# Self-attention of a fused transformer block: the sum of the rotary embedding on GpSimd, V projected behind the cosines, and new orders for the stage

## What is computed

```python
def _rope(x, sin, cos):
    xe = x[..., ::2]; xo = x[..., 1::2]
    return jnp.stack((xe*cos - xo*sin, xe*sin + xo*cos), axis=-1).reshape(x.shape)

attn_in = _adaln(x, cond, ...)
q = _heads(attn_in @ wq); k, v = jnp.split(attn_in @ wkv, 2, axis=-1)
q = _rope(q, ...); k = _rope(_heads(k), ...)
a = softmax(einsum('bhnd,bhmd->bhnm', q, k) * DH**-0.5)
x = (heads_joined(a @ v)) @ wo + bo + x
```

## Time and profile before

| what | value |
|---|---|
| median of the runs | 2123.01 us |
| the profiled execution: its own time, its span | 2127.94 us, 2126.2 us |
| TensorE, VectorE, ScalarE, GpSimd busy over the span | 94%, 76%, 47%, 55% |
| the self-attention stage | from 34.03 us (first projection) to 438.86 us (last add) |
| granted TensorE clock over the program | 0.97 of full speed |

### The profile page before, as it was taken

The page is one execution under the profiler, slowest core; times in us unless marked ns, Lnnn a source line. Parts: engine busy times, 40 slices in busy tenths (PEclk is TensorE's granted clock), DMA queues, the critical chain, the costliest instruction groups (busy, mean ns, idle before and its releaser), DMA issues.

```text
span 2126.2 us, 53808 instructions
## 1 busy us (share of the span) xinstructions
PE 2008.8 (94%) x20816; PEld 1346.6 (63%) x20816; DVE 1622.6 (76%) x2362; ACT 990.0 (47%) x1606; POOL 1174.4 (55%) x721
## 2 busy tenths in 40 slices
PE   5899999879699999999999999999999999999987
PEld 2666667622166666666666766767666776776653
DVE  3788888836578888888887888888788887888832
ACT  2344444424244445445445545444554544554533
POOL 1344444400056667677677667667666766766760
PEclk8999999979799999999999999999999999999999
DMA  3522222100011111111111111111111111111100
GB/s 112 165 80 75 81 79 82 54 0 1 32 55 54 47 54 60 47 54 57 50 52 55 54 49 54 58 47 54 60 47 54 59 48 53 55 53 52 48 22 20
DMA packets 109750, 118.69 MB, mean 56 GB/s; under 512 B 26432, under 2 KB 74688, under 8 KB 109248
## 3 DMA queue, kind: packets, MB, share of 16 engines
q1 hardware_dynamic: 109504, 115.27, 16.4%
HBM read 36.52 MB, written 1.05 MB: 18 GB/s over the span
## 4 chain that ended last, share of the span: by engine, by line
PE 68%; POOL 13%; issue 11%; DMA 3%; DVE 3%; ACT 2%; SPq 0%; POOLq 0%; ACTq 0%; DVEq 0%
PE S L1089 18%; PE OB L1101 16%; PE PB L1036 8%; PE PB L1047 8%; PE S L1062 6%; POOL psum_acc L503 4%; POOL psum_acc L470 4%; POOL KL L463 4%; PE S L885 2%; PE PB L1110 2%; DMA qswapped<-qturned 2%; PE PB L1026 1%; PE PB L872 1%; PE PB L1120 1%; PE PB L1071 1%
## 5 line engine op out<-in xcount | busy, mean ns | idle before, releaser
L503 POOL TENSOR_TENSOR psum_acc<-psum_acc,P 124x1024 f32<-124x1024 f32 (+1 forms) x320 | 689.4, 2154 | 92.9 <-ACT P L628 75.1
L628 ACT ACTIVATE P<-S 124x1024 f32<-124x1024 f32 (+1 forms) x448 | 431.3, 963 | 465.9 <-PE S L1089 465.1
L817 DVE TENSOR_REDUCE mxc<-S 128x2 f32<-128x1024 f32 x384 | 469.1, 1222 | 89.4 <-PE S L1062 88.6
L1101 PE MATMUL OB<-P,V 124*64 124x256 f32 (+1 forms) x3328 | 429.4, 382 | 0.0
L496 POOL TENSOR_TENSOR psum_acc<-P 124x1024 f32<-124x1024 f32 x64 | 152.3, 2379 | 331.4 <-ACT P L628 331.4
L1101 PEld LDWEIGHTS OB<-P,V 124*64 124x64 f32 (+1 forms) x3328 | 224.5, 137 | 131.0 <-issue 40.8
L1089 PE MATMUL S<-QH,KH 64*124 64x256 f32 (+1 forms) x1664 | 254.2, 301 | 3.0 <-ACT P L628 3.0
L783 DVE TENSOR_TENSOR turned<-PB,rope 128x512 f32<-128x512 f32 (+1 forms) x256 | 146.0, 570 | 120.6 <-PE PB L1036 120.2
L1089 PE MATMUL S<-QL,KH 64*124 64x256 f32 (+1 forms) x1664 | 234.8, 277 | 0.0
L1089 PE MATMUL S<-MX,share 64*124 64x256 f32 (+1 forms) x1664 | 234.7, 277 | 0.0
L1089 PE MATMUL S<-QH,KL 64*124 64x256 f32 (+1 forms) x1664 | 234.5, 277 | 0.0
(11 more groups left out here) (118 smaller groups left out, 3241.2 us busy)
## 6 DMA issues: line engine op xcount, KB each, us to landing
swapped<-turned SPq DMA_DIRECT2D x512, 128.0 KB, 2.1
kv_w<-sa_kv_dram SPq DMA_DIRECT2D x64, 128.0 KB, 2.3
qswapped<-qturned SPq DMA_DIRECT2D x128, 64.0 KB, 1.9
kv_w<-ca_kv_dram SPq DMA_DIRECT2D x64, 96.0 KB, 2.2
ctxT_all<-ctxT_dram SPq DMA_DIRECT2D x8, 600.4 KB, 5.3
q_w<-sa_wq_dram SPq DMA_DIRECT2D x64, 64.0 KB, 2.0
q_w<-ca_wq_dram SPq DMA_DIRECT2D x64, 64.0 KB, 2.0
o_w<-ca_wo_dram SPq DMA_DIRECT2D x64, 64.0 KB, 2.1
```

The costliest lines, as they stand in the source:

```text
L503: pool.tensor_tensor(acc, acc, P_of(J, c)[0:rows, :, 0:w], ALU.add).then_inc(x.acc, 1)
L628: act.activation(P_of(J, c)[0:rows, :, 0:w], SP[0:rows, :, 0:w], ACT.Exp, scale=SCALE).then_inc(x.e, 1)
L817: dve.tensor_reduce(mxc[:, t, :, c:c + 1], MP[:, :, 0:w], AX.X, ALU.max).then_inc(x.am, 1)
L1101: ins = pe.matmul(OB[half(h), 0:N], Vb[J % 2][0:w, t, half(h)], P_of(J, c)[0:w, h, k * N:(k + 1) * N], start=(t == 0), stop=(t == len(a_.t ...
```

## The change

Three edits, all in self-attention:
1. The rotation's sum `r` leaves VectorE's list and becomes an instruction of GpSimd. `c` no longer works in place in PSUM: it writes its product from the bank into `QK[J % 2]` in SBUF, and takes over the wait for `l` of the step before the last, which frees that buffer. `r` then adds `swapped` to `QK` in place.
2. `v` waits for `c` of its step instead of `r`.
3. All tables but SyncE's are new. The projection leads by two iterations instead of three, `v` by one instead of two, `a` by one instead of two and `m` by none instead of one; the output product and its add lag by two instead of one.

```diff
     SELF = Stage("sa",
-                 "qk+3 sum+-1 p+-1 s v+2 a+2 m+1 o+-1",
-                 "r+2 am+1 t+3 rc+-1 dv+-1 c+3 ad+-1",
-                 "ve+1 mr h+2 oe+-1 e",
-                 "l+2 f",
+                 "qk+2 v+1 o+-2 m a+1 p+-1 sum+-1 s",
+                 "ad+-2 t+2 c+2 am+1 rc+-1 dv+-1",
+                 "ve+1 mr oe+-1 e h+2",
+                 "l+1 r+2 f",
                  "w+3 x+2")
...
+                def rotate(J, _):
+                    i = J % SLOTS
+                    wait(pool, z.c, J + 1)
+                    wait(pool, z.swap[i], J // SLOTS * 32 + 32)
+                    pool.tensor_tensor(QK[J % 2][:, :], QK[J % 2][:, :], swapped[i][:, :], ALU.add).then_inc(z.r, 1)
...
                 def cosines(J, _):
-                    wait(dve, z.t, J + 1)
-                    bank = halves(KB[J % 2][:, :])
-                    dve.tensor_tensor(bank, bank, both(ropeq[:, 0:N]), ALU.mult).then_inc(z.c, 1)
-
-                def rotate(J, _):
-                    i = J % SLOTS
-                    wait(dve, z.c, J + 1)
-                    wait(dve, z.swap[i], J // SLOTS * 32 + 32)
                     wait(dve, z.l, J - 1)
-                    dve.tensor_tensor(QK[J % 2][:, :], KB[J % 2][:, :], swapped[i][:, :], ALU.add).then_inc(z.r, 1)
+                    dve.tensor_tensor(halves(QK[J % 2][:, :]), halves(KB[J % 2][:, :]), both(ropeq[:, 0:N]), ALU.mult
+                                      ).then_inc(z.c, 1)
...
                 def project_v(J, _):
                     loaded(J)
-                    wait(pe, z.r, J + 1)
+                    wait(pe, z.c, J + 1)
```

More of the change, by code:

```diff
@@ L470, in fold @@
                     pool.tensor_tensor(added_up(J), P[:, :, 0:N], P[:, :, N:2 * N], ALU.add).then_inc(z.f, 1)
-                run_steps(SELF, in_order(SELF.pool, {"l": low_parts, "f": fold}))
+                run_steps(SELF, in_order(SELF.pool, {"r": rotate, "l": low_parts, "f": fold}))
             def cross():
@@ L757, in add @@
                         dve.tensor_tensor(x_b, x_b, XB[:, 0:N], ALU.add).then_inc(z.added, 1)
-                run_steps(SELF, in_order(SELF.dve, {"t": turn, "c": cosines, "r": rotate, "am": maximum,
+                run_steps(SELF, in_order(SELF.dve, {"t": turn, "c": cosines, "am": maximum,
                                                     "rc": invert, "dv": divide, "ad": add}))
```

## The result

The changed kernel takes 2111.76 us, the median of five runs (2104.18 to 2112.91), against 2122.61 for the kernel before (2121.08 to 2126.22): a ratio of 0.9941, with a 95% interval of 0.9921 to 0.9961. That is 10.9 us or 0.5% faster. The forecast was 2100.5 us, 22.5 us faster. The result lies outside the forecast's own range of 2095 to 2106 us and 0.24 us inside the end of the wide one, 2090 to 2112. Measured again on another occasion the kernel took 2113.56 us, ratio 0.9936 (0.9912 to 0.9960).

What follows compares the result with a forecast made beforehand. VectorE bounds the kernel at 5.19 us a step, TensorE 4% behind. Gains: 52 x 0.24 = 12.5, 7 x 0.72 = 5.0, fill 3, late copies 2, together 22.5 us: 2100.5 us against 2123.0; 8-in-10 range 2090 to 2112.

Steps and rivals of the forecast that it cites:

- TensorE's floor: Sum of TensorE's group distances in one self-attention step, start to start, kept for the new order: 4.91 us.
- The bank's loop: Shared bank's loop in a step, from maxima's rows through scores, products, sums, inverse and division to TensorE: 4.92 us.
- the exponential's: Loop in a step from scores through exponential, high parts behind it on ScalarE, and back to TensorE: 4.94 us.
- The signs that I had named: In the new profile: maxima 4.95 us apart, 9.2 at outputs, GpSimd's pass 1.28, TensorE above 97% of a 44 us batch.
- the signs of being wrong: Scores for the maximum regularly waiting for high parts, GpSimd's passes above 1.3 us, or a first batch not shorter.
- Late copies: Exchanged-row copies in self-attention: 0.28 us late at no cost, fifteen late ones give 2 us; bounds -3 and +4.
- The fill: Start of self-attention: the second step's turn no longer stands behind the first rotation; gain 3 us, between 1 and 5.
- The end: End of self-attention, where nothing overlaps: no change expected.
- Rival 1: Handovers between engines eat the gain: with 0.15 us more the step is 5.10 us, time 2109 us; chance 0.2.
- Rival 2: TensorE is no floor: the copy's loop decides the step at 4.81 us, 7 us more gain, 2093 us; chance 0.1.
- Rival 3: One bound exchanged for another: the step stays at 5.19 us, only the start of the stage gains, 2120 us; chance 0.07.
- Rival 4: VectorE and GpSimd's added pass take turns at SBUF: step 5.75 us, slower at 2159 us; chance 0.05.

Runs made afterwards that it cites:

- e_noinv: On `e_lead`, VectorE's inverse of the sums replaced by a multiplication with a column: 2088.78 us, ratio 0.9856 to the kernel before.
- e_nocopy: Changed kernel, but the rotation adds the turned tile and doesn't wait for the copy with exchanged rows, which still runs: 2093.97 us, ratio 0.9850.
- e_lead: Changed kernel with projection, turn, cosines and copy one iteration further ahead and a third QK buffer: 2097.13 us, ratio 0.9857 to the kernel before.
- after_again: The changed kernel, unchanged, measured once more on another occasion: 2113.56 us, ratio 0.9936 to the kernel before.
- e_dverot: Changed kernel with the rotation's sum back on VectorE, the new orders kept: 2133.66 us, ratio 1.0034 to the kernel before.
- e_oldorder: Changed kernel's edits 1 and 2 with the leads and order of the kernel before, only GpSimd's table changed: 2101.48 us, ratio 0.9901.
- e_fewer: On `e_lead`, one of the three products of the scores left out, 4 of a step's 16 matmuls: 2098.55 us, ratio 0.9902.

## Why the prediction was right, and where it was not

**Right.** VectorE set the step before, and the move freed it. TensorE's floor: forecast 4.91, measured 4.90 to 4.92 in `e_noinv`. The step: forecast 4.95, measured 4.95. The output step: 9.24, measured 9.23. GpSimd's pass: 1.28, measured 1.277 in the median; its handover to ScalarE: 0.05, measured 0.03. The bank's loop, forecast at 4.92, was mis-sized by 0.03 and sits on top instead of the exponential's: from the products to the sums it is 0.91 us and not 0.86, and the sums' matmuls take 0.60 and not 0.63. The forecast of 4.95 stood on the exponential's 4.94, so that it is exact to the hundredth is luck.

The signs that I had named came in part. One of the signs of being wrong came: the scores for the maximum waited for the high parts, 17 times and 14.4 us from 100 to 400 us. TensorE was not above 97% of a batch of 44 us; the best batch of the changed kernel is this one, 96.7%:

```profile
148.50:193.40 44.90, 43.41 (x480) 30.78 (x480) 37.54 (x42) 20.83 (x40) 30.23 (x24) 1.00 0.26 84
```

**Wrong, and the cause of the missing half: "Late copies".** I took +2 us, with -3 as the lower bound; it was -9. The step that failed is the count. I let the fifteen late copies of before stay fifteen, as if lateness were weather. From the twelfth step on it was 8 before and is 20 now. The order of before issues its copies as the scores begin (166.49 and 166.29 us in the earlier trace rows), and its long packets mostly start 0.5 to 1.2 us ahead of an issue; the new order issues them behind the maxima's rows, at 169.45 us in the step above, and there 17 long packets fell on a copy. The slack was 0.32 to 0.38 us, near the 0.28 that I had; the second half of the fault is that I called it a reserve and did not ask what the late copies behind the earlier trace rows, up to 1.7 us each from the twelfth step on, would do to it. What a late copy costs by the slack is shown step by step, and that the copies' lateness is the cause by `e_nocopy` and `e_lead`. That instruction packets make them late rests on the coincidences counted above.

**The fill** was forecast at 3 us, and about 2.7 came: the first maximum stands 1.9 us nearer to the first projection, the four steps of the fill gain 0.24 us each, and the excess up to the twelfth maximum is 0.2 us more than before.

**The end** gained 5.4 us where I forecast none. In the profile of before TensorE ran there at a lower clock: the last output product took 5.62 us where it took 3.67 in the middle and in the changed kernel's end. The windows from the last maximum on, before and after; the second number from behind the counts is the granted clock:

```profile
417.20:439.30 22.10, 15.48 (x108) 9.35 (x108) 8.21 (x8) 3.96 (x7) 3.27 (x3) 0.77 0.00 1
```

```profile
407.50:424.10 16.60, 11.08 (x108) 7.43 (x108) 8.20 (x8) 3.59 (x6) 3.81 (x4) 1.00 0.00 1
```

TensorE is granted 0.77 of full speed on the average there before, its full speed after. The execution decides at least a part of that: in the second profile of the changed kernel (`after_again`) the granted clock is 0.90 there, the last output product takes 5.03 us and the end 17.9. The ends of the other kernels took 15 to 21 us. Without the end, the table's gains come to 11.4 us, near the 10.9 of the medians.

**The rivals.** Rival 1, handovers, named nearly the right time (2109) for the wrong reason: the handovers are about as short as I took them, and the step is 4.95 and not 5.10. That the result falls into the wide range, which was drawn for rivals 1 and 2 and not for late copies, is luck. Rival 2, TensorE no floor, has fallen with `e_noinv`. Rival 3, a step still at 5.19, has fallen with the step of 4.95. The rule that I weighed there (the Trainium skill, Perfetto Trace Analysis, Identifying the Most-Contended Engine) gives TensorE room at 69% of weight loads; the measurement decides against it for this mix of matmuls: in `e_noinv`, with weight loads at 69%, the step is the sum of TensorE's own distances. Rival 4, mutual exclusion, doesn't happen in the changed kernel, but `e_dverot` shows that it exists once both inputs of VectorE's sum lie in SBUF.

**Open.** Why the long packets start mostly at two distances from the issue, and by what a packet delays a copy. I did not try to move the packets away from the copies by design, and no run has the copies without the packets.

## What to carry to other kernels

When an engine is freed, write down for each transfer in the loop how late it may be, and compare that with the lateness that the trace of before has already, not with its mean; a schedule that is tight to 0.3 us loses to disturbances of 1 to 2 us whatever its ideal pace. One more buffer and one more iteration of lead, with no more work for any engine, gave more than the reordering itself (`e_lead`, 15 to 16 us under the changed kernel). Try the move alone before the new orders: here `e_oldorder`, with a slower step, beat the full change by 10 to 12 us. And before a match between a forecast and a total is believed, its terms should be compared one by one: here the step was right, and the total was off by half of the gain.

## What the runs showed of the hardware

- Packets of an instruction queue run beside the kernel's own transfers, one of 16384 bytes for each 256 to 258 matmuls and weight loads of TensorE, and take 0.9 to 1.6 us. A pair of 128 KB copies with one between issue and landing landed 0.7 to 2.3 us later in the changed kernel (17 of 17), but not in `e_fewer` where the packet started 2.15 us or more behind the issue (8 of 8 on time). If it starts 0.3 to 0.55 us behind the first issue, SyncE's second issue takes 1.24 to 1.65 us instead of 0.60.
- A VectorE sum with both inputs in SBUF and a GpSimd pass that reads SBUF lengthen each other: 1.26 became 1.72 us, 0.68 became 1.53 and up to 1.725 (`e_dverot`). Beside VectorE's products with one input in PSUM GpSimd's passes kept 1.26 to 1.30 us.
- VectorE's product from PSUM and SBUF costs the same into SBUF (0.68 us) as into PSUM (0.69, rows 2).
